# A transformer block on one core: the last batch's attention in two passes over the queries, and a new set of planning constants

## The chip, the cores and the metric

The kernel runs on one core of a Trainium2 chip. The metric is the device time of one execution, in microseconds (us); less is better. TensorE is called PE, VectorE DVE, ScalarE ACT, GpSimd POOL and SyncE SP, as in the profile. All DMAs but the indirect ones are issued from SP's queue; the indirect gathers and scatters are issued from POOL's.

## The reference, cut to what matters

Input x is 8 batches of 1024 tokens with 256 features. Per batch: layer norm, causal attention with 16 heads of 16 features, in which every value row is scaled by a gate computed from its token (a small network), output projection and residual; then layer norm and a mixture of experts (8 experts of 128 hidden units, 2 of them chosen per token by a grouped gate, and a shared expert of 256 hidden units) with its residual.

```python
Q = (x @ Wq + bq); K = (x @ Wk + bk); V = (x @ Wv + bv)        # 16 heads of 16
logits = einsum('bqhd,bkhd->bhqk', Q, K) * scale               # causal
attn = softmax(logits); gated = attn * gate[:, None, None, :]
x = x + einsum('bhqk,bkhd->bqhd', gated, V) @ Wo + bo
...
h = silu(x @ w1[e]) * (x @ w3[e]);  y = sum_e ew[t, e] * h @ w2[e]
shared = silu(x @ sg) * (x @ su) @ sd;  out = x + y + shared
```

## The kernel before

**A list scheduler writes the order.** `plan_work` adds items: each has an engine, an estimated duration, a due time, the items it needs, PSUM banks and, on PE, a tiling (`FULL`, `ROWS`, `COLS`). `Plan.run` simulates the engines greedily: of the items of an engine that can start now it takes the one with the least due time, with `SAME_TILING` added to the due time of an item that would change PE's tiling, and it never leaves an engine idle for an item that comes later. The result is a fixed order of instructions for each engine. Items of one kind (the two letters of their name) keep the order in which they were added. `LATER` shifts the due times of whole kinds; `SWITCH` and `EXPOSED` are charged to PE items. These numbers never reach the chip: only the order does.

**Attention.** The 16 heads go in 4 groups of 4, the queries in 2 chunks of 512 (c = 0 and 1). For a group and chunk: `LD` loads stacked queries and keys from DRAM (`load_stacks`, L965); `M` computes scores on PE (L1908) only to find each row's maximum with `MR` on DVE (L1549); `MT`, `MN` and `SM` turn, negate and move the maxima into the query stack (L1928, L1340, L972); `QK` computes transposed scores (L1941), `EX` exponentials on ACT (L1358), `MK` clears the causal corner on POOL (L1175), `PV` multiplies with the values on PE (L1961), `OE` and `SO` copy and store the sums (L1369, L978). Chunk 0 sees keys 0 to 511 and needs 5 scores items of the 18 of a group, all of them on the diagonal; chunk 1 sees all keys and needs 13. Every batch runs group by group, chunk 0 then chunk 1. There are 4 query halves (`Q_HALVES`) and 5 key halves (`K_HALVES`) in SBUF; chunk 1 uses the key half that chunk 0 loaded together with its own. The load of a group's chunk waits for the scores of the same chunk two groups before.

**Feed-forward.** The attention output of a batch is taken in quarters of 256 tokens. Once all four groups have stored a chunk, `CL`, `CR` and `CV` invert the softmax sums (L986, L1561, L990); then for each quarter `CO` loads (L1004 to L1007), `CP` scales on POOL (L1184, L1185), `CW` projects (L1970), a layer norm follows, `CT` transposes (L1978) and `CG` computes the gate (L1993). A unit of the feed-forward is `EU` (12 or 6 matmuls, L2071), `HT` (2 transposes, L2081) and `ED` (6 matmuls, L2102), with ACT and DVE work between them. In batches 0 to 6 a quarter runs 2 units (the shared expert), and the chosen experts run as units over tokens gathered by expert (`pair`: `XL` L1023, `XT` L2034, `YC` L1448, `YS` L1033), and `mix` brings them back: `RL` L1042, the two gathers `GY` on POOL (L1219), `CM` on ACT (L1294), `CB` and `CC` on POOL (L1227, L1232), `SY` L1046. The last batch has nothing behind it to hide this in, so its quarters run all 10 units densely: 40 units in all. `quarter_due`, `pairs_due` and `mix` give the due times; `LOOKS` sorts quarters and pairs into the one order in which their units run.

Around the end, then, the order is: the last batch's group 3, chunk 0, then chunk 1; its quarters 0 and 1 (tokens of chunk 0) and 2 and 3 (chunk 1); in between, the pairs of batch 6 and the mixing of batches 4 to 6.

Of the kernel before, what the change touches and what calls it, by code (L numbers as in the profile page):

```python
# [13 lines left out]
P = 128  # L14
B, S, E = 8, 1024, 256
H, DH = 16, 16
KE = E // P
# [49 lines left out]
LAST_MAX = [max(u for u in range(NMAX) if MAXU[u][0] == c) for c in range(CHUNKS)]  # L67
FFN_CHUNKS = 6
# [30 lines left out]
Q_HALVES, K_HALVES = 4, 5  # L99
ROWS_OF_HEAD = 64  # L100
# [9 lines left out]
SWITCH, EXPOSED = 100, 90  # L110
PERIOD, KEEPS = 3413, 0.58
SAME_TILING = 12000
# [9 lines left out]
FIRST = 50_000  # L122
SHARE_FROM, SHARE_TO, PAIRS_FROM, MIX_LONG = 0.12, 0.5, 0.72, 0.15
# [6 lines left out]

def quarter_due(n, q):
    return at(n + 1) + T * (SHARE_FROM + (SHARE_TO - SHARE_FROM) * q / QS)
# [45 lines left out]
def max_parts(u):  # L178
# [3 lines left out]
    for qt in qts:  # L182
# [7 lines left out]
LATER = {"AC": 8000, "AQ": -1000, "AX": 7000, "CB": 6000, "CC": -41000, "CG": 3000, "CJ": 2000, "CL": -8000,  # L190
# [33 lines left out]
class Plan:  # L224
# [16 lines left out]
    def run(self):  # L241
# [10 lines left out]
        while left:  # L252
# [76 lines left out]
def plan_work():  # L329
# [8 lines left out]
    def step_due(n, g, s):  # L338
        return at(n, g) + GROUP_T * step_at[s] // step_at[NSTEP]
# [66 lines left out]
    def values(n, g):  # L406
        add("POOL", ("VA", n, g), 1437, at(n, g) - 4000, [("PK", K_HALVES), ("GL", n), ("PV", n - 1, g, NSTEP - 1)])

    def maxima(n, g):
        gi = n * GROUPS + g  # L410
        older = divmod(gi - 2, GROUPS)
        begin = at(n, g) - GROUP_T * 0.98
        for c in range(CHUNKS):
            m = g // (GROUPS // KE)
            add("SP", ("LD", n, g, c), 4 * ISSUE, begin - GROUP_T * (1.0 - 0.3 * c),
# [13 lines left out]
            if c:  # L429
                add("DVE", ("MJ", n, g), 95, due, last)  # L430
                last = [("MJ", n, g)]
# [1713 lines left out]
```

## Time and profile before

| | |
|---|---|
| median of 3 runs | 1799.14 us (1796.13 to 1805.52) |
| the profiled execution | 1808.59 us, its span 1806.6 us |
| PE busy | 1653.0 us (91%) |
| DVE busy | 1292.4 us (72%) |
| ACT busy | 1081.9 us (60%) |
| POOL busy | 811.8 us (45%) |
| mean granted TensorE clock | 0.962 of full speed |

Busy time is the union of an engine's instructions. The chain of waits is followed back from the last instruction; windows are stretches of the span, counted from its start.

### The profile page before, as it was taken

To read this page: it belongs to the slowest core of one execution; us is meant where nothing else is said; L and a number is where in the kernel's file an instruction comes from. 1 tells how busy PE (TensorE), PEld (TensorE's weight loads), DVE (VectorE), ACT (ScalarE), POOL (GpSimd) and SP (SyncE) were. 2 spreads that over 40 slices of the span, in tenths; PEclk is the share of its full clock that TensorE was granted. 3 is DMA by queue.
4 is the path that set the end of the run, shared out by engine and by line. 5 is a ranking of instruction groups with operands and counts; after the bars stand their busy time and mean duration, and the time that the engine had idled before them with its cause. 6 is when DMAs were issued, how large, how long until landed. Compare 5 with 4: busy or idle time off the path is not lost.

```text
span 1806.6 us, 34673 instructions
## 1 busy us (share of the span) xinstructions
PE 1653.0 (91%) x12785; PEld 982.5 (54%) x12785; DVE 1292.4 (72%) x2528; ACT 1081.9 (60%) x1808; POOL 811.8 (45%) x1390
## 2 busy tenths in 40 slices
PE   7798989989988999899998989999999889999888
PEld 3344446435544566455654555555564557666677
DVE  5776767967795777777785757877688666963655
ACT  3466756665655655675656755586556765568432
POOL 5234533463345221632237863363207773157760
PEclk9699999999998999999998999999999999999999
DMA  5556655554445532644545665453535675336440
GB/s 151 158 156 194 176 169 152 182 153 124 125 127 147 158 104 87 174 113 120 159 118 151 185 194 152 127 162 108 147 93 172 198 197 159 97 129 199 135 122 13
DMA packets 192708, 261.25 MB, mean 145 GB/s; under 512 B 19616, under 2 KB 127264, under 8 KB 192544
## 3 DMA queue, kind: packets, MB, share of 16 engines
q1 hardware_dynamic: 181792, 229.67, 44.0%
q0 software_dynamic: 10752, 29.37, 5.6%
q8 instruction: 105, 1.72, 0.4%
q14 instruction: 59, 0.48, 0.1%
HBM read 130.98 MB, written 127.40 MB: 143 GB/s over the span
## 4 chain that ended last, share of the span: by engine, by line
PE 54%; DVE 14%; DMA 8%; ACT 8%; POOL 8%; issue 5%; SPq 3%; another core or an unknown queue 0%; POOLq 0%; ACTq 0%; DVEq 0%
PE ps_all L1961 10%; PE ps_all L2071 10%; DVE mx L1549 7%; PE ps_all L1941 6%; PE ps_all L1908 6%; PE ps_all L2102 5%; PE ps_all L1892 4%; ACT probs L1358 4%; PE ps_all L1878 3%; PE ps_all L1970 3%; POOL xs_s L1207 2%; PE ps_all L2081 2%; PE ps_all L2034 1%; DMA rr<-r_s 1%; DMA out<-rr 1%
## 5 line engine op out<-in xcount | busy, mean ns | idle before, releaser
L1549 DVE TENSOR_REDUCE mx<-ps_all 128x2 f32<-128x1024 f32 (+2 forms) x640 | 619.0, 1006 | 132.5 <-PE ps_all L1908 74.4
L1358 ACT ACTIVATE probs<-ps_all 128x1024 f32<-128x1024 f32 x576 | 571.8, 1028 | 218.0 <-PE ps_all L1941 209.9
L1175 POOL TENSOR_SCALAR_AFFINE_SELECT probs<-probs 128x256 f32<-128x256 f32 (+1 forms) x448 | 190.9, 443 | 495.5 <-ACT probs L1358 491.3
L1961 PE MATMUL ps_all<-probs,vaug 128*32 128x512 f32 (+3 forms) x3072 | 319.4, 516 | 21.9 <-POOL probs L1175 15.3
L1908 PE MATMUL ps_all<-k_st,q_st 63*128 63x512 f32 (+3 forms) x1536 | 269.3, 401 | 48.0 <-ACT probs L1358 16.3
L1941 PE MATMUL ps_all<-q_st,k_st 64*128 64x512 f32 (+3 forms) x1536 | 265.6, 401 | 29.3 <-ACT probs L1358 9.9
L1908 PEld LDWEIGHTS ps_all<-k_st,q_st 63*128 63x128 f32 x1536 | 135.1, 193 | 163.7 <-issue 52.2
L1941 PEld LDWEIGHTS ps_all<-q_st,k_st 64*128 64x128 f32 x1536 | 130.9, 191 | 158.9 <-issue 67.2
L2071 PE MATMUL ps_all<-w_hi,x2h 128*128 128x512 f32 (+1 forms) x480 | 168.2, 350 | 4.3 <-DVE x2l L1598 2.5
L1804 DVE SCALAR_TENSOR_TENSOR act_t<-act_t,ps_all 128x256 f32<-128x256 f32 x168 | 70.4, 419 | 123.4 <-ACT act_t L1421 110.9
L2071 PE MATMUL ps_all<-w_lo,x2h 128*128 128x512 f32 (+1 forms) x480 | 157.0, 327 | 0.0
L2071 PE MATMUL ps_all<-w_hi,x2l 128*128 128x512 f32 (+1 forms) x480 | 157.0, 327 | 0.0
L1421 ACT ACTIVATE act_t<-ps_all 128x256 f32<-128x256 f32 x168 | 64.6, 385 | 151.3 <-PE ps_all L2071 122.2
L1961 PEld LDWEIGHTS ps_all<-probs,vaug 128*32 128x32 f32 x3072 | 73.2, 110 | 131.6 <-issue 89.4
L1207 POOL DMA_INDIRECT xs_s<-xnb,slot_u x112 | 111.6, 996 | 42.9 <-issue 39.8
L1219 POOL DMA_INDIRECT yab<-ys_s,slot_u x112 | 108.3, 967 | 33.0 <-issue 20.2
L2102 PE MATMUL ps_all<-w_hi,h_hi 128*128 128x256 f32 (+1 forms) x336 | 109.5, 326 | 7.7 <-DVE h_lo L1831 6.9
L2071 PEld LDWEIGHTS ps_all<-w_hi,x2h 128*128 128x128 f32 x480 | 90.8, 189 | 27.6 <-issue 19.7
L1878 PE MATMUL ps_all<-wvd,xt 128*128 128x384 f32 x256 | 96.9, 506 | 1.8 <-issue 0.9
L2071 PEld LDWEIGHTS ps_all<-w_hi,x2l 128*128 128x128 f32 x480 | 90.9, 189 | 8.4
L1831 DVE TENSOR_TENSOR h_lo<-ps_all,h_hi 128x256 fp32r<-128x256 f32 x168 | 70.0, 419 | 35.1 <-ACT h_hi L1436 32.7
L2102 PE MATMUL ps_all<-w_lo,h_hi 128*128 128x256 f32 (+1 forms) x336 | 94.3, 281 | 0.0
(195 smaller groups left out, 2849.8 us busy)
## 6 DMA issues: line engine op xcount, KB each, us to landing
qk_s<-qh SPq DMA_DIRECT2D x116, 256.0 KB
q_st<-qk_s SPq DMA_DIRECT2D x128, 192.0 KB
k_st<-qk_s SPq DMA_DIRECT2D x128, 192.0 KB
xs<-xs_s SPq DMA_DIRECT2D x72, 256.0 KB
ys_s<-ysb SPq DMA_DIRECT2D x72, 256.0 KB
o_s<-o_sb SPq DMA_DIRECT2D x64, 256.0 KB
qk_s<-ql SPq DMA_DIRECT2D x57, 256.0 KB
xs_s<-ysb SPq DMA_DIRECT2D x20, 512.0 KB, 6.0
```

What stands on the lines that cost most here:

```text
L1175: last = nc.gpsimd.affine_select(out=block, in_=block, compare_op=ALU.is_ge, fill=0.0, base=0, pattern=[[0, heads], [1, P]], channel_multi ...
L1207: nc.gpsimd.indirect_dma_start(xs_s[i % 2], bass.IndirectOffsetOnAxis(ap=slot_u[:, n % 4, a, t:t + 1], axis=0), xnb[:, t, :], None).then_i ...
L1219: nc.gpsimd.indirect_dma_start(yab[:, t % 2, a, :], None, ys_s[SET_OF[n] % 2], bass.IndirectOffsetOnAxis(ap=slot_u[:, n % 4, a, t:t + 1], ...
L1358: nc.scalar.activation(to, of, ACT.Exp, scale=DH ** -0.5).then_inc(freed[release[item][0]], 1)
L1549: last = nc.vector.tensor_reduce(to[:, :, p, qt % QPC], both[:, :, at:at + keys], X_AXIS, ALU.max)
L1878: last = mm(bank(item)[:, 0:E + DP], xt[:, k, tt * P:(tt + 1) * P], wvd[:, k, :], start=(k == 0), stop=(k == KE - 1))
L1892: last = mm(bank(item), w[:, k, m * P:(m + 1) * P], xt[:, k, :], start=(k == 0), stop=(k == KE - 1))
L1908: last = mm(bank(item, j)[:, to:to + keys], q_st[r, q_half(n, g, c), p, qt % QPC * P:(qt % QPC + 1) * P], k_st[r, k_half(n, g, kc), p, 0:k ...
L1941: last = mm(bank(item, j)[:, to:to + cols], k_st[r, k_half(n, g, kt // QPC), a, kt % QPC * P:(kt % QPC + 1) * P], q_st[r, q_half(n, g, c), ...
L1961: last = mm(bank(first)[32 * h:32 * h + 32, q0 - c * CHUNK:], vaug[:, kt, g, h * VW:h * VW + 32], probs[:, s % 2, h, at:at + cols], start= ...
L2071: last = mm(bank(item)[:, to], x[:, buf, k, t * P:(t + 1) * P], w[:, k, cs], start=(k == 0 and j == 0), stop=(k == KE - 1 and j == 2))
L2102: last = mm(bank(first)[:, t * E:(t + 1) * E], h[:, z % 2, i * P:(i + 1) * P], w[:, cs], start=(item == first and i == 0 and j == 0), stop ...
```

## The change

1. The last batch's attention goes over chunk 0 of all four groups first, then over chunk 1 of all four. The list of (batch, group, chunk) in the new order is `VISITS`; all counters that semaphores are compared with are taken from positions in it.
2. In the last batch chunk 1 can no longer use the keys of chunk 0 where they were, so its load fetches both halves: 6 DMAs in place of 4 for each of 4 visits. `FREED_BY` names the visit whose scores must be done before a load may overwrite its buffers.
3. Quarters 0 and 1 of the last batch get earlier due times (`EARLY_FROM`, `EARLY_STEP`), and so does the inversion of their softmax sums.
4. The planner's costs change (`SWITCH`, `EXPOSED` and where they are charged, `SAME_TILING`), and `LATER` is replaced by a table with 91 kinds in place of 42.

```diff
+VISITS = ([(n, g, c) for n in range(B - 1) for g in range(GROUPS) for c in range(CHUNKS)]
+          + [(B - 1, g, c) for c in range(CHUNKS) for g in range(GROUPS)])
+VISIT_NO = {visit: v for v, visit in enumerate(VISITS)}
+STEP_NO, SCORE_NO, MASK_NO, MAX_NO = {}, {}, {}, {}
+for n, g, c in VISITS:
+    for s in range(FIRST_STEP[c], LAST_STEP[c] + 1):
+        STEP_NO[n, g, s] = len(STEP_NO)
+        for p in range(SCORES[s]):
+            SCORE_NO[n, g, s, p] = len(SCORE_NO)
+            if DIAGONAL[s]:
+                MASK_NO[n, g, s, p] = len(MASK_NO)
+    for u in range(NMAX):
+        if MAXU[u][0] == c:
+            MAX_NO[n, g, u] = len(MAX_NO)
+STEP_AT = list(STEP_NO)
...
+KEYS = [(v, kc) for v, (n, g, c) in enumerate(VISITS) for kc in range(c if n < B - 1 else 0, c + 1)]
+KEY_NO = {}
+for v, (n, g, c) in enumerate(VISITS):
+    for kc in range(c + 1):
+        KEY_NO[v, kc] = KEYS.index((v, kc) if (v, kc) in KEYS else (VISIT_NO[n, g, kc], kc))
+
+
+def freed_by(v):
+    last = {}
+    for (w, _), k in KEY_NO.items():
+        if w < v:
+            last[k % K_HALVES] = max(last.get(k % K_HALVES, 0), w)
+    own = [k % K_HALVES for k, (w, _) in enumerate(KEYS) if w == v]
+    return max([v - Q_HALVES] + [last.get(k, -1) for k in own])
+
+
+FREED_BY = [freed_by(v) for v in range(len(VISITS))]
...
-SWITCH, EXPOSED = 100, 90
+SWITCH, EXPOSED = 130, 60
 PERIOD, KEEPS = 3413, 0.58
-SAME_TILING = 12000
+SAME_TILING = 7000
...
+EARLY_FROM, EARLY_STEP = 0.95, 0.1
...
+def visit_at(n, g, c):
+
+    first = sum(SCORES[:FIRST_STEP[1]])
+    if n < B - 1:
+        return at(n, g) + c * GROUP_T * first // NSCORE
+    return at(n) + (c * T * first + g * GROUP_T * (NSCORE - first if c else first)) // NSCORE
+
+
 def quarter_due(n, q):
+    if n == B - 1 and q < QS // CHUNKS:
+        return at(n) + T * (EARLY_FROM + EARLY_STEP * q)
...
-LATER = {"AC": 8000, "AQ": -1000, "AX": 7000, "CB": 6000, "CC": -41000, "CG": 3000, "CJ": 2000, "CL": -8000,
...
+LATER = {"AB": 8000, "AC": 29000, "AE": 15000, "AG": -53000, "AN": 7000, "AQ": -1000, "AR": 26000, "AS": 46000,
...
                 if tile != tiling:
-                    ns += SWITCH + EXPOSED * (tile != COLS)
-                    tiling = tile
-                elif idle and tile != COLS:
-                    ns += min(EXPOSED, idle)
+                    ns, tiling = ns + SWITCH, tile
+                elif item[0] not in ("PV", "ED"):
...
+        load = begin - GROUP_T * (1.0 - 0.3 * c)
+        if n == B - 1:
+            begin = visit_at(n, g, c) - GROUP_T * (0.75 if c else 0.6)
+            load = begin - GROUP_T * 0.4
+        m = g // (GROUPS // KE)
+        user = FREED_BY[v]
+        free = [("QK",) + VISITS[user][:2] + (LAST_STEP[VISITS[user][2]], SCORES[LAST_STEP[VISITS[user][2]]] - 1)] if user >= 0 else []
+        add("SP", ("LD", n, g, c), (4 + 2 * (n == B - 1 and c)) * ISSUE, load,
+            [("PK", min(v + 1, K_HALVES - 1)), ("SQ", n, c, 2 * m), ("SQ", n, c, 2 * m + 1)] + free,
+            lands=9000 if n else 5000)
+        units = [u for u in range(NMAX) if MAXU[u][0] == c]
...
             early = at(n + 1) - (GROUP_T * 0.4 if c == 0 else 0)
+            if n == B - 1 and c == 0:
+                early = visit_at(n, 0, 1) + GROUP_T * 0.1
...
-        for g in range(GROUPS):
+        for g in range(GROUPS if n < B - 1 else 0):
             values(n, g)
-            maxima(n, g)
+            for c in range(CHUNKS):
+                maxima(n, g, c)
             if g + n * GROUPS:
                 pn, pg = divmod(n * GROUPS + g - 1, GROUPS)
                 for s in range(NSTEP):
                     attention(pn, pg, s)
-        if n:
+        if n and n < B - 1:
             rest(n - 1)
-    for s in range(NSTEP):
+    begun = VISIT_NO[B - 1, 0, 0]
+    for v in range(begun, len(VISITS)):
+        if v < begun + GROUPS:
+            values(*VISITS[v][:2])
+        maxima(*VISITS[v])
+        for n, g, c in VISITS[v - 2:v] if v == begun else VISITS[v - 1:v]:
+            for s in range(FIRST_STEP[c], LAST_STEP[c] + 1):
+                attention(n, g, s)
+    for s in range(FIRST_STEP[1], NSTEP):
         attention(B - 1, GROUPS - 1, s)
+    rest(B - 2)
     rest(B - 1)
...
-                if gi >= 2:
-                    sp.wait_ge(s_full, (gi - 2) * NSCORE + sum(SCORES[:LAST_STEP[c] + 1]))
-                cs = slice(c * CHUNK, (c + 1) * CHUNK)
-                for kind in range(2):
+                if FREED_BY[v] >= 0:
+                    on, og, oc_ = VISITS[FREED_BY[v]]
+                    sp.wait_ge(s_full, SCORE_NO[on, og, LAST_STEP[oc_], SCORES[LAST_STEP[oc_]] - 1] + 1)
+                for kind, part in [(0, c)] + [(1, kc) for w, kc in KEYS if w == v]:
+                    cs = slice(part * CHUNK, (part + 1) * CHUNK)
                     rows = qk_s[bass.ds(((n * 2 + kind) * H + g * GROUP) * TERMS, GROUP * TERMS), :]
                     rows = rows.rearrange("(p j r) s -> j r p s", j=2, r=TERMS)
                     for j in range(2):
                         r = slice(ROWS_OF_HEAD * j, ROWS_OF_HEAD * j + TERMS)
-                        to = q_st[r, q_half(n, g, c), :, :] if kind == 0 else k_st[r, k_half(n, g, c), :, :]
+                        to = q_st[r, q_half(n, g, c), :, :] if kind == 0 else k_st[r, k_half(n, g, c, part), :, :]
                         sp.dma_start(to.bitcast(F32), rows[j][:, :, cs]).then_inc(st_in[gi % 2][c], 16)
```

## Rows read from the trace of the kernel before

**Rows 1.** The page: busy time of each engine, share and instructions.
```profile
PE 1653.0 (91%) x12785; PEld 982.5 (54%) x12785; DVE 1292.4 (72%) x2528; ACT 1081.9 (60%) x1808; POOL 811.8 (45%) x1390
```
**Rows 2.** Windows: stretch, its length, busy of each engine (instructions), clock, DMA.
```profile
100.00:1455.00 1355.00, 1259.02 (x10011) 711.73 (x10009) 1002.49 (x1867) 846.72 (x1347) 593.68 (x1014) 0.97 0.52 148
1455.00:1660.00 205.00, 193.04 (x1635) 131.82 (x1635) 141.70 (x269) 136.68 (x247) 105.24 (x155) 0.99 0.53 155
```
**Rows 3.** Windows, the same columns, ten us each around the two gaps.
```profile
1660.00:1670.00 10.00, 7.28 (x55) 4.65 (x55) 2.35 (x6) 5.43 (x11) 6.73 (x9) 0.90 0.59 173
1670.00:1680.00 10.00, 5.14 (x27) 3.37 (x26) 2.02 (x7) 3.98 (x8) 7.04 (x11) 0.84 0.60 159
1680.00:1690.00 10.00, 9.08 (x39) 6.59 (x39) 6.17 (x19) 3.29 (x10) 6.21 (x7) 0.75 0.56 179
1690.00:1700.00 10.00, 8.53 (x46) 6.72 (x45) 7.84 (x31) 5.36 (x15) 8.18 (x12) 1.00 0.31 95
...
1740.00:1750.00 10.00, 6.52 (x21) 4.21 (x22) 2.24 (x7) 3.50 (x9) 6.55 (x10) 0.66 0.58 172
1750.00:1760.00 10.00, 8.09 (x43) 6.50 (x42) 8.54 (x28) 2.48 (x7) 4.17 (x4) 1.00 0.15 51
1760.00:1770.00 10.00, 10.00 (x55) 8.74 (x54) 6.13 (x21) 3.81 (x11) 1.07 (x3) 0.83 0.01 2
```
**Rows 4.** Timeline of PE at the first gap: start, length, instructions, idle before.
```profile
1672.40 0.64 PE L1961 MATMUL ps_all<-probs,vaug 128*32 128x256 f32 x8
1672.97 1.13 PE L1970 MATMUL ps_all<-wo,oc 128*128 128x256 f32 x4
1678.96 1.18 PE L1978 MATMUL ps_all<-ident,xnb 128*128 128x128 f32 x4 [4.86 <-ACT xnb L1315]
...
1682.31 0.63 PE L2071 MATMUL ps_all<-w_hi,x2h 128*128 128x512 f32 x1
```
**Rows 5.** Chain of waits near the end: start, length, what.
```profile
1790.60 1.37 PE ps_all L2071 x6
1791.97 0.22 PE ps_all L2081 x2
1792.19 0.71 PE ps_all L2102 x6
1792.90 1.38 PE ps_all L2071 x6
```
**Rows 6.** Timeline of SP: stores of the last batch's sums, and the loads after them.
```profile
1457.55 0.47 SPq L978 DMA_DIRECT2D o_s<-o_sb  x1
1475.16 0.58 SPq L978 DMA_DIRECT2D o_s<-o_sb  x1
1522.80 0.43 SPq L978 DMA_DIRECT2D o_s<-o_sb  x1
...
1625.49 0.33 SPq L978 DMA_DIRECT2D o_s<-o_sb  x1
1638.80 0.33 SPq L978 DMA_DIRECT2D o_s<-o_sb  x1
...
1673.72 0.32 SPq L978 DMA_DIRECT2D o_s<-o_sb  x1
1686.97 0.61 SPq L990 DMA_DIRECT2D li_s<-rows_of  x1
```
**Rows 7.** Timeline of SP: from quarter 0's sums to its loads.
```profile
1652.07 0.60 SPq L990 DMA_DIRECT2D li_s<-rows_of  x1
1655.86 0.64 SPq L1004 DMA_DIRECT2D oc<-o_s  x1
```
**Rows 8.** Timeline of POOL: quarter 0's and quarter 3's scaling.
```profile
1666.87 1.27 POOL L1184 TENSOR_TENSOR oc<-oc,lb 128x512 f32<-128x512 f32 x1
...
1754.22 1.34 POOL L1184 TENSOR_TENSOR oc<-oc,lb 128x512 f32<-128x512 f32 x1
```
**Rows 9.** Timeline of SP: group 3's stacks loaded, its last maxima moved.
```profile
1573.63 0.80 SPq L965 DMA_DIRECT2D q_st<-qk_s  x2
1574.48 0.90 SPq L965 DMA_DIRECT2D k_st<-qk_s  x2
...
1617.48 1.32 SPq L972 DMA_DIRECT2D q_st<-rows_of  x2
```
**Rows 10.** The page, costliest groups: maxima on DVE.
```profile
L1549 DVE TENSOR_REDUCE mx<-ps_all 128x2 f32<-128x1024 f32 (+2 forms) x640 | 619.0, 1006 | 132.5 <-PE ps_all L1908 74.4
```
**Rows 11.** Timeline of PE: a feed-forward unit cut by attention scores.
```profile
1659.65 0.28 PE L2071 MATMUL ps_all<-w_hi,x2l 128*128 x1
1659.86 0.50 PE L1941 MATMUL ps_all<-q_st,k_st 64*128 64x384 f32 x4
1660.29 0.39 PE L2102 MATMUL ps_all<-w_hi,h_hi 128*128 x1
```

More of the change, by code:

```diff
@@ L406, in values, with maxima @@
     def values(n, g):
-        add("POOL", ("VA", n, g), 1437, at(n, g) - 4000, [("PK", K_HALVES), ("GL", n), ("PV", n - 1, g, NSTEP - 1)])
-    def maxima(n, g):
+        add("POOL", ("VA", n, g), 1437, visit_at(n, g, 0) - 4000, [("PK", K_HALVES), ("GL", n), ("PV", n - 1, g, NSTEP - 1)])
+    def maxima(n, g, c):
         gi = n * GROUPS + g
         older = divmod(gi - 2, GROUPS)
+        v = VISIT_NO[n, g, c]
         begin = at(n, g) - GROUP_T * 0.98
-        for c in range(CHUNKS):
-            m = g // (GROUPS // KE)
-            add("SP", ("LD", n, g, c), 4 * ISSUE, begin - GROUP_T * (1.0 - 0.3 * c),
-                [("PK", min(gi * CHUNKS + c + 1, K_HALVES - 1)), ("SQ", n, c, 2 * m), ("SQ", n, c, 2 * m + 1), ("QK",) + older + (LAST_STEP[c], SCORES[LAST_STEP[c]] - 1)],
-                lands=9000 if n else 5000)
-            units = [u for u in range(NMAX) if MAXU[u][0] == c]
-            for u in units:
-                _, p, kc, qts = MAXU[u]
-                blocks = len(qts) * (1 if p is not None else PAIRS)
-                due = begin + GROUP_T * 0.9 * u / NMAX
-                add("PE", ("M", n, g, u), 240 if kc < c else 310 if blocks == 1 else 445, due,
-                    [("BT",), ("LD", n, g, c), ("MT",) + older + (c,)], 2, ROWS)
-                add("DVE", ("MR", n, g, u), sums(2 * sum(part[1] for part in max_parts(u)) * blocks // len(qts)) + 65 * len(qts), due + 1000, [("M", n, g, u)],
-                    frees=(("M", n, g, u), None))
-            due += 1500
-            last = [("MR", n, g, units[-1])]
-            if c:
-                add("DVE", ("MJ", n, g), 95, due, last)
-                last = [("MJ", n, g)]
-            add("PE", ("MT", n, g, c), 60, due, last, 1, FULL)
-            add("ACT", ("MN", n, g, c), 160, due, [("MT", n, g, c)] + ([("SM",) + divmod(gi - 1, GROUPS) + (c,)] if gi else []),
-                frees=(("MT", n, g, c), None))
-            add("SP", ("SM", n, g, c), 2 * ISSUE, due, [("MN", n, g, c)], lands=2600)
@@ new lines, in maxima @@
+        units = [u for u in range(NMAX) if MAXU[u][0] == c]
+        for u in units:
+            _, p, kc, qts = MAXU[u]
+            blocks = len(qts) * (1 if p is not None else PAIRS)
+            due = begin + GROUP_T * 0.9 * (u - units[0] * (n == B - 1)) / NMAX
+            add("PE", ("M", n, g, u), 240 if kc < c else 310 if blocks == 1 else 445, due,
+                [("BT",), ("LD", n, g, c), ("MT",) + older + (c,)], 2, ROWS)
+            add("DVE", ("MR", n, g, u), sums(2 * sum(part[1] for part in max_parts(u)) * blocks // len(qts)) + 65 * len(qts), due + 1000, [("M", n, g, u)],
+                frees=(("M", n, g, u), None))
@@ L437, in attention @@
+        due += 1500
+        last = [("MR", n, g, units[-1])]
+        if c:
+            add("DVE", ("MJ", n, g), 95, due, last)
+            last = [("MJ", n, g)]
+        add("PE", ("MT", n, g, c), 60, due, last, 1, FULL)
+        add("ACT", ("MN", n, g, c), 160, due, [("MT", n, g, c)] + ([("SM",) + divmod(gi - 1, GROUPS) + (c,)] if gi else []),
+            frees=(("MT", n, g, c), None))
+        add("SP", ("SM", n, g, c), 2 * ISSUE, due, [("MN", n, g, c)], lands=2600)
     def attention(n, g, s):
@@ L1954, in sums @@
                 if DIAGONAL[s]:
-                    pe.wait_ge(p_masked, gi * MASKS + sum(SCORES[i] for i in range(s + 1) if DIAGONAL[i]))
+                    pe.wait_ge(p_masked, MASK_NO[n, g, s, SCORES[s] - 1] + 1)
                 else:
```

69 lines of the change are left out of this document (34 added, 35 removed), and 16 rows, old and new, of the table LATER.

## The prediction

> **What bounds the kernel now.** The page's list of busy times comes first: PE is busy 91% of the span, the next engine, DVE, 72% [rows 1]. So PE's work is the bound as long as something is ready for it, and time is lost only where PE waits or runs at its low clock. Windows over long stretches say where: from 100 to 1455 us PE is idle for 1355 - 1259 = 96 us, from 1455 to 1660 us (nearly all of the last batch's attention) for 12 us only, at a granted clock of 0.99 [rows 2]. Windows of ten us behind that show two gaps. From 1660 to 1700 us PE is idle for 2.7 + 4.9 + 0.9 + 1.5 = 10.0 us, and the granted clock falls to 0.75 of full, so a part of it at 1.2 instead of 2.4 GHz; from 1740 to 1770 us it is idle for 3.5 + 1.9 = 5.4 us with the clock down to 0.66 [rows 3]. The clock's share is roughly (1 - clock) times the busy time of each row: 0.7 + 0.8 + 2.3 = 3.8 us in the first, 2.2 + 1.7 = 3.9 us in the second. Together the two gaps cost 10.0 + 5.4 + 3.8 + 3.9 = 23.1 us.
>
> The timeline shows what the first one is. The last PV of the attention and the projection of quarter 0 end at about 1674 us; then PE has nothing for 4.86 us, until ACT's normalised rows of quarter 0 arrive, and quarter 0's first dense unit begins at 1682.3 us [rows 4]. All 40 dense units of the last batch lie behind the attention. Once they flow they repeat every 2.31 us (1790.60 to 1792.90) with PE full: 1.37 us of EU, 0.22 of HT, 0.71 of ED [rows 5]. Nothing in the units themselves can be shortened by an order; only the gaps can.
>
> Quarters 0 and 1 need only chunk 0 of the four groups. Its last store is issued at 1638.8 us, because group 3's chunk 0 comes so late [rows 6].
>
> **The change, part by part.**
>
> *The order of the last batch.* The stores of sums, taken in turn (chunk 1 of batch 6, then chunks 0 and 1 of batch 7's groups), give the length of a visit: 17.6 us for group 0's chunk 0 and 47.6 for its chunk 1, 34.9 for group 3's chunk 1; over the whole, 1673.7 - 1457.6 = 216 us, or 54 a group, of which 5/18 = 15 is chunk 0 and 13/18 = 39 chunk 1 [rows 6]. With all chunks 0 first, they are done at 1457.6 + 4 x 15 = about 1518 us, 120 us before the present 1638.8. Quarters 0 and 1 can then run anywhere from about 1550 us on: 20 units, 46 us of PE work, that need not wait for the end. PE's amount of work does not shrink by this. What it can give back is the gaps: both lie where the chain of a quarter (load, scaling, projection, norm, gate) ran with no unit ready, and now 20 units can stand there. I take all of the 23.1 us as removed, and count what is late next as a term of its own.
>
> *Idle time within the attention.* 12 us of it are left [rows 2], and a unit that is ready can fill such holes: 5 units at most. Bounds 0 and -12; the holes are short and spread, nearest to half: -6.
>
> *What is late next: quarters 2 and 3.* They still need the very last chunk. From the last PV (1673.0) to the inverted sums' store (1687.0 + 0.6) are 14.6 us [rows 4, 6]; from quarter 0's such store to its first load 3.8 us [rows 7]; from there to its scaling on POOL 11.0 us [rows 7, 8], some of which is POOL busy with the mixing (lower bound 7); from the scaling to the first unit 1682.3 - 1666.9 = 15.4 us [rows 4, 8]. The chain is 41 to 45 us. It must be covered by units of quarters 0 and 1 that are still unspent. Their due times (0.95 and 1.05 of the batch's length) stand just before and just behind the attention's last steps, so the planner gives attention the first place and spends units early only where PE would idle, about 5. 15 x 2.31 = 35 us of cover remain, and the last pairs of batch 6 add a little. Uncovered: 41 to 45 minus 35, 6 to 10 us; with the clock's fall behind such a gap (nearly 4 us of 14 in the first one) and a few us covered by pairs, I take +9. If no unit were left it would be over 40; this is the first rival below.
>
> *Keys loaded twice, and their buffers.* 4 visits issue 6 loads in place of 4; two take 0.90 us of SP's queue [rows 9], so 3.6 us of issue in all, spread over 150 us in which SP has long pauses: nothing, and if that cover were gone, under 1 us a visit. Behind these two on SP stand the moves of maxima and the stores of sums, which would be late by the same 0.9 us. The wait matters more. Two key halves a visit in a ring of 5 means that a visit's load waits for the scores of the visit two before. Up to now a chunk 1 load could be issued 54 + 15 = 69 us before its scores were due; now, 39 us (34.9 for the last ones). Group 3's load and the last move of its maxima stand 1617.5 - 1573.6 = 44 us apart, unhurried [rows 9]; the least is 13 maxima of 1.006 us on DVE [rows 10] plus about 10 us for load, turn and move, 25 us in all (this 10 is an estimate from the pieces of the chain above: each pass through DRAM took 4 to 8 us). So the chain fits if DVE gives it priority, and is late by up to 10 us a visit if it does not. While it is late PE still has units. Bounds 0 and +15; I take +3, nearest to the row of 25 us needed against 35 given.
>
> *Switches of tiling.* Dense units ran unbroken behind the attention; among scores and values PE changes its tiling around each piece. In the row where a unit's last matmul (pace 0.12 us) is followed by scores, about 0.1 us goes at each of the two changes [rows 11]. A unit has 3 pieces, so at most 6 changes, 0.6 us. For 5 to 8 units +3 to +5; for all 20, +12; I take +4, since the due times leave most units behind the attention.
>
> The Trainium skill bears on this place. TensorEngine Tiling (Array Packing), Key Properties, says that a change of tiling mode drains TensorE, and names no price. The row above shows such a boundary at about 0.1 us; by the row the sum is the one below; by a drain that every piece pays in full it would be that of the rival on switches.
>
> *Costs and due times of the whole plan.* The first seven batches are reordered as well, with no change of work. Here the trace shows only the pool: 96 us of idle PE between 100 and 1455 us [rows 2]. One thing can be tested: the old charges add to 1370 + 140 + 692 = 2202 ns for a unit without idle time, the new ones to 2322, and the trace has 2.31 us [rows 5]. The new charges describe a full PE better, so an order made by them has a fair chance to be better on the chip; but a table of shifts up to 87 us is fitted to the planner, not to the chip. Bounds -20 (a fifth of the idle time) and +20; I take -5, near to nothing.
>
> **The sum.** -23.1 - 6 + 9 + 3 + 4 - 5 = -18 us. Against the profiled execution, 1808.6 us, that is 1790.6, or -1.0%. That execution lies 9.5 us above the median of the runs shown, 1799.1, so the same share gives a median of 1781 us.
>
> **The rivals.**
>
> *The cover is spent too early* (the slower side). Batch 7 has no projections of a next batch to fill PE with, and the planner is greedy: each stall in the chunk 1 visits takes a unit. With k units left at the last PV, 45 - 2.31 k us are exposed, and the sum is -23 - 12 + 45 + 2 (clock) + 3 + 12 (switches of 20 units) - 5 (retuning) - 2.31 k = 22 - 2.31 k. It decides from k = 9.5: fewer left is slower than before. With 4 left, +13: 1812. For it: the units are ready at 1550 us, 120 us early. Against it: only 12 us of idle time are there to take them [rows 2], and their due times. Chance 0.13.
>
> *The key ring stalls each chunk 1 visit.* Three visits late by 5 us that units do not fill: +15 in place of +3: -6, so 1793. For it, 44 us unhurried against 35; against it, DVE's 72%. Chance 0.14.
>
> *Every unit pays dear switches.* All 20 units spread over the attention, each of 6 changes at twice the row's 0.1 us: +24 in place of +4, with the idle time filled whole, -12 in place of -6. The sum is -4, 1795. For it, that the row shows a boundary only where the next weights were at hand; against it, that attention and pairs mix in this way already at 94% busy [rows 2]. Chance 0.10.
>
> *The retuning is worth more than the order.* -20 in place of -5: -33, 1766. For it, 96 us of idle PE that an order could use. Chance 0.15.
>
> *The change does not do what it says*: quarters 0 and 1 are due but held by POOL, whose gathers and additions for the mixing stand before the scaling (it ran at 1666.9 though its loads were issued at 1655.9 [rows 7, 8]). Then the tail stays as it was and only the retuning is left, around 1799 and on either side of it. Chance 0.08.
>
> **How the numbers follow.** The forecast, 1781, has a chance of 0.40 with a range of its own from 1770 to 1792. Faster and slower by 0.5% (9 us, about what a measurement here tells from no change) are below 1790 and above 1808. Faster: most of the forecast's 0.40 (0.36), the retuning 0.15, half of the ring's and the switches' together 0.12, a little of the others 0.04: 0.67. Slower: the spent cover 0.10, the last rival and the bad side of the retuning 0.05: 0.15. The rest, 0.18, is no change. The range for 8 in 10 goes from 1757, the retuning rival and its own spread, to 1806, where the ring, the switches and the unchanged tail lie within it and most of the spent cover does not.
>
> **What would show it.** In the trace after: the last store of chunk 0 near 1520 us in place of 1638.8; dense units (L2071 in its form with 6 matmuls) before the last PV; PE's idle time between the last PV and the end under 12 us; a single gap, if any, in front of quarter 2's first unit; the load of a chunk 1 visit issued right after the scores of the visit two before, and PE at 0.94 or more busy there. A gap of over 20 us behind the last PV would show the first rival; PE or ACT waiting for the move of the maxima the second; PE busy time up by 10 us with no new idle time the third; the same gaps with the end earlier, the fourth.

## The result: slower by 1.5%, and the profile after

The changed kernel takes 1827.57 us in the median of 4 runs (1820.24 to 1834.68); the kernel before, run beside it, 1800.97 us. The ratio is 1.0146 [1.0112, 1.0181]. The forecast was 1781, the range ended at 1806, and the chance given to slower was 0.15. The profiled executions lie closer together than the medians: 1820.2 us after and 1808.6 before, so the two traces hold only 12 of the 27 us by which the medians differ.

The page of the changed kernel, busy times, answers to [rows 1]:

```profile
PE 1650.7 (91%) x12726; PEld 980.8 (54%) x12726; DVE 1284.9 (71%) x2528; ACT 1085.6 (60%) x1808; POOL 813.1 (45%) x1390
```

PE does the same work in both kernels; what was added is idle time: 14 us, while its busy time fell by 2. Windows of the changed kernel (stretch, length, busy time of PE, PEld, DVE, ACT and POOL with instructions, granted clock, DMA share, GB/s): up to the last batch's first sums, from there to its last PV, and the tail.

```profile
0.00:1462.00 1462.00, 1331.15 (x10344) 747.91 (x10344) 1048.27 (x1971) 890.13 (x1408) 636.23 (x1146) 0.96 0.51 147
1462.00:1702.00 240.00, 215.15 (x1758) 144.71 (x1757) 162.19 (x329) 151.49 (x279) 133.39 (x192) 0.99 0.52 156
1702.00:1819.00 117.00, 104.40 (x634) 88.21 (x632) 74.41 (x229) 44.01 (x123) 43.44 (x54) 0.97 0.28 87
```

The same three stretches of the kernel before:

```profile
0.00:1457.00 1457.00, 1336.03 (x10455) 750.20 (x10455) 1067.97 (x1986) 892.93 (x1420) 640.04 (x1153) 0.96 0.52 148
1457.00:1673.00 216.00, 202.38 (x1695) 138.04 (x1695) 143.23 (x275) 140.70 (x255) 112.52 (x164) 0.98 0.53 155
1673.00:1807.00 134.00, 114.62 (x640) 94.26 (x636) 81.25 (x268) 48.23 (x135) 59.29 (x75) 0.93 0.29 88
```

Length minus PE's busy time is its idle time. The tail lost 17 us of length and 6.8 of idle time (19.4 to 12.6), as a change of that kind should do. The attention before it grew by 24 us, of which 11.2 is idle time (13.6 to 24.9) and the rest units that moved into it. So the last batch takes 7 us more as a whole, and the first seven batches 5. Those 5 say too little: fewer matmuls lie in that stretch (10344 records against 10455), and PE's idle time in it grew by 10 us, from 121.0 to 130.9. So the seven batches whose attention order nobody meant to change hold a large part of the new idle time. This pair of traces cannot say where the other 15 us of the medians are; runs side by side on one chip could.

SP's timeline of the changed kernel (start, length, queue, line, transfer, count) answers to [rows 6, 7]; "..." marks rows left out:

```profile
1534.44 0.34 SPq L1046 DMA_DIRECT2D o_s<-o_sb  x1
...
1702.33 0.32 SPq L1046 DMA_DIRECT2D o_s<-o_sb  x1
...
1715.90 0.60 SPq L1058 DMA_DIRECT2D li_s<-rows_of  x1
...
1723.98 0.39 SPq L1082 DMA_DIRECT2D out<-x  x1
...
1726.24 0.62 SPq L1072 DMA_DIRECT2D oc<-o_s  x1
```

The first row is the last store of a chunk 0, at 1534 us in place of 1639; the second the last store of a chunk 1. The last three are the store of chunk 1's inverted sums, which quarters 2 and 3 need, the store of quarter 0's result, and quarter 2's first load; they come back below.

### The profile page after: what moved, and what is told of

The parts are those of the page before. It is cut to its first block, busy times and chain, and to the rows that moved or that the text cites. A ratio compares the mean times of both kernels' runs of the same rounds, so it can differ in the third digit from the quotient of the medians.

```text
span 1818.4 us, 34577 instructions
## 1 busy us (share of the span) xinstructions
PE 1650.7 (91%) x12726; PEld 980.8 (54%) x12726; DVE 1284.9 (71%) x2528; ACT 1085.6 (60%) x1808; POOL 813.1 (45%) x1390
## 4 chain that ended last, share of the span: by engine, by line
PE 46%; DMA 13%; DVE 12%; ACT 9%; POOL 7%; SPq 6%; issue 5%; another core or an unknown queue 1%; POOLq 0%; DVEq 0%; ACTq 0%
PE ps_all L2136 9%; PE ps_all L2026 8%; PE ps_all L2167 5%; DVE mx L1614 5%; PE ps_all L2006 5%; PE ps_all L1973 5%; ACT probs L1425 4%; PE ps_all L1957 4%; DMA qk_s<-ql 3%; POOL xs_s L1275 2%; PE ps_all L1943 2%; PE ps_all L2035 2%; PE ps_all L2146 2%; SPq L1004 1%
## 5 line engine op out<-in xcount | busy, mean ns | idle before, releaser
L2026 PE MATMUL ps_all<-probs,vaug 128*32 128x512 f32 (+3 forms) x3072 | 319.0, 510 | 16.3 <-POOL probs L1243 12.7
L2026 PEld LDWEIGHTS ps_all<-probs,vaug 128*32 128x32 f32 x3072 | 70.6, 110 | 118.0 <-issue 80.5
L1501 ACT CAST h_hi<-ps_all 128x256 fp32r<-128x256 f32 x168 | 62.1, 372 | 80.6 <-PE ps_all L2146 74.9
```

What stands on the lines that cost most here:

```text
L2026: last = mm(bank(first)[32 * h:32 * h + 32, q0 - c * CHUNK:], vaug[:, kt, g, h * VW:h * VW + 32], probs[:, STEP_NO[n, g, s] % 2, h, at:at ...
```

## Experiments

Two theories stood at the start. **A**: the new constants made a worse order of the first seven batches. **B**: the loss is in the last batch, from its order or its key ring. Neither had it alone, and **C** came after the first four runs: a detail of the new due times that seemed to change nothing. **D** and **E** are about one wait of the tail, and come last. Each kernel ran 4 to 10 times. Ratios are to the kernel before on the same chip, with a 95% interval; they are estimated from the runs and are not the quotients of the two medians. The kernels of one heading shared a chip. Code cuts leave lines out where "..." stands.

### First chip (the kernel before: 1791.66 us)

`e1` is the new order with the old charges and shifts.

```diff
-SWITCH, EXPOSED = 130, 60
+SWITCH, EXPOSED = 100, 90
...
-SAME_TILING = 7000
+SAME_TILING = 12000
...
-                elif item[0] not in ("PV", "ED"):
...
+                elif idle and tile != COLS:
...
```

The table `LATER` is the old one of 42 kinds again.

> The new order of the last batch with the old planning constants: SWITCH, EXPOSED and SAME_TILING and the table LATER are those of the kernel before. Theory A (the loss lies in the new constants, which reorder all eight batches; the order of the last batch is a gain): 1780 to 1795 us against 1801, last store of attention sums before 1685 us. Theory B (the order of the last batch itself loses, through the ring of five key halves: PE runs dry in front of the last chunk 1 visit): 1810 to 1830, the last store near 1700.

Measured: 1804.18 us, 1.0063 [1.0032, 1.0094]. Slower, but by less than half of the loss, and in the range of neither theory.

`e2` is the opposite: the kernel before, only with the new charges, `SAME_TILING` and table.

> The old order of the last batch with the new charges and the new table LATER. Theory A: slower than before, 1810 to 1825. Theory B: within 0.5% of before or faster, 1785 to 1808. The end of batch 6's attention (store of its last sums), 1457.6 us before and 1462.4 after the change, lies near 1462 in both.

Measured: 1767.76 us, 0.9882 [0.9841, 0.9922]. The constants alone were faster here, so A fell; that they were faster by this much neither theory had said. (The size did not come back on two other chips, e9 and e15 below.)

`e3` is the changed kernel with the old table `LATER` and the new charges.

> The changed kernel with the old table LATER, but the new charges (SWITCH, EXPOSED, SAME_TILING). Theory A: if the table is what loses, near e1_reorder_only; if the charges are, near the changed kernel, 1820 to 1830. Theory B: near the changed kernel, and again a wait of PE for the maxima of a chunk 1 visit.

Measured: 1806.32 us, 1.0088 [1.0061, 1.0115]. Not to be told apart from e1: without the new table the loss is as small as without all new constants, although e2 shows no loss from the table by itself.

`e4` is e1 without the double load: in the last batch chunk 1 loads one key half and uses it for both, so its scores come from keys partly not the right ones, with the same instructions on PE. The lines that follow from this one (which half is read, what is waited for, the planned length of the load) change with it.

```diff
-KEYS = [(v, kc) for v, (n, g, c) in enumerate(VISITS) for kc in range(c if n < B - 1 else 0, c + 1)]
+KEYS = [(v, c) for v, (n, g, c) in enumerate(VISITS)]
...
```

> As e1_reorder_only, but in the last batch chunk 1 loads one key half and uses it in place of both (wrong keys, same matmuls, 4 DMAs a visit in place of 6), so that the ring of five is no limit: the load may be issued as soon as the queries' buffer is free. Theory A: within 4 us of e1. Theory B: 8 to 15 us faster than e1, with the last chunk 1 visits 35 to 39 us long and no wait of PE for a maximum.

Measured: 1797.29 us, 1.0025 [1.0003, 1.0047]; against e1 0.4% or 7 us less, the intervals just overlapping. In the profiles the stretch of attention shrinks from 245 to 236 us and the tail is 108 us in both. So the key ring probably costs something, between the +3 of the forecast and the +15 of the second rival, though not clear of noise; the planned order of the last batch differs between e1 and e4 too. Both theories' ranges (within 4 us, 8 to 15 us) were missed.

### Second chip (1800.24 us): the rounding

That A and B were each too small left what e1, e3, e4 and the changed kernel share and e2 has not. The new function of due times adds up two integer divisions where one stood:

```diff
-        return at(n, g) + GROUP_T * step_at[s] // step_at[NSTEP]
+        c = STEPS[s][0]
+        return visit_at(n, g, c) + GROUP_T * (step_at[s] - step_at[FIRST_STEP[c]]) // step_at[NSTEP]
```

For batches 0 to 6 the two mean the same time, but two divisions round down twice: for `QK` of batch 0, step 4, it gives 73332 ns where it was 73333. So 768 of the attention's 1792 score, exponential, mask and PV items, all in chunk 1's steps, become due 1 ns earlier. What follows was worked out from the plans of e2 and e6, which have the new constants and differ in nothing else. The first order that differs is a tie in batch 0: score item (0, 0, 8, 1) is taken on PE ahead of the maxima item (0, 1, 13), not behind it. From there the greedy planner goes another way through all batches: 1592 of PE's 2503 items stand in another place (by 4.3 places in their mean, 72 at most), 1313 of DVE's 2136. Making all `M` items due 1 ns later has exactly the same effect.

The planner's own simulation shows the loss as well: its last item starts at 1645.0 us in e2's plan and at 1661.6 in e6's, at 1649.4 with exact due times (e7) and 1668.5 in the changed kernel. And it shows that this is no even draw. Moving the due time of one kind at a time by 1000 ns either way lengthens e2's plan in 41 of the 44 cases that change its length, by 8.9 us in the median, and shortens the changed kernel's in 36 of 44. So the new constants look fitted to the exact due times, and the rounding takes the plan off that fit. These are plans and were not run. With the old constants the rounding lengthens the plan less, from 1671.0 to 1675.4 us.

`e5` puts that rounding, and nothing else, into the kernel before; `e6` puts it into e2.

```diff
-        return at(n, g) + GROUP_T * step_at[s] // step_at[NSTEP]
+        first = step_at[FIRST_STEP[STEPS[s][0]]]
+        return at(n, g) + GROUP_T * first // NSCORE + GROUP_T * (step_at[s] - first) // NSCORE
```

> The kernel before with one thing of the change: the due times of the attention steps are computed with the new formula's two whole-number divisions in place of one, which makes those of a third of the attention items 1 ns smaller. Ties in the list scheduler then fall otherwise, and from 74 us of the plan on the order of all batches is another one. Theory C (much of the loss is this reshuffle, which nobody chose): 8 us or more away from before, near e1_reorder_only (0.6% slower). Theory B (the last batch's order is the loss): within 0.3% of before.

Measured: 1810.47 us, 1.0060 [1.0040, 1.0080]. With the old constants the rounding alone costs 0.6%, all that e1 lost.

> As e2_retune_only (new charges and table, old order of the last batch), with the new formula's rounding, 1 ns in a third of the due times. Theory C: well above e2's ratio of 0.988, 1.000 or more, so that only the rest to 1.0146 is the last batch's order. Theory B: 0.988 within 0.3%.

Measured: 1819.61 us, 1.0117 [1.0057, 1.0177]. With the new constants it comes to most of the whole loss (e2, its partner, ran on another chip; the pair on one chip is e9 and e11).

`e7` takes it out of the changed kernel by the edit below; `e8` also gives quarters 0 and 1 and their inversion the old due times.

```diff
     def step_due(n, g, s):
         c = STEPS[s][0]
+        if n < B - 1:
+            return at(n, g) + GROUP_T * step_at[s] // step_at[NSTEP]
         return visit_at(n, g, c) + ...
```

> The changed kernel with the old formula for the due times of batches 0 to 6, so that its order is the one of e2_retune_only until near the end of batch 6, and differs only by the new order of the last batch. Theory C: a large part of the way from 1.0146 back to e2's 0.988, 0.995 or less. Theory B: 1.010 or more, with the same waits in the last batch as after the change.

Measured: 1792.78 us, 0.9966 [0.9940, 0.9991].

> As e7_after_exact, but quarters 0 and 1 of the last batch have their old due times, behind the attention. If interleaving quarter 0 with the attention costs (it delays the last chunk 1 visits), 3 to 8 us faster than e7; if it fills holes as forecast, slower by as much. The order of visits is the same in both.

Measured: 1790.15 us, 0.9945 [0.9923, 0.9966]. One added `if` in the planner (e7), without any arithmetic on the chip changed, turns 1.5% slower into a little faster. No effect of the early due times is seen: the intervals of e7 and e8 overlap, though by the plans 6 units of quarter 0 begin ahead of the last PV in e7 and none in e8.

### Third chip (1803.61 us): two by two

All four have the new constants; old or new formula for batches 0 to 6, old or new order of the last batch. e9 is e2 again, e10 is e7, e11 is e6, e12 the changed kernel.

> The kernel of e2 once more, so that the four corners (formula old or new, order of the last batch old or new, all with the new constants) stand on one chip with the same runs of before. Theory C (the reshuffle is the loss): 0.988 of before again. If e2 owed its time to its chip: 0.993 or more.

> The kernel of e7 once more: old formula, new order of the last batch. Theory C: 0.997 of before; its distance to e9, some 0.8%, is then the price of the new order of the last batch. If that price came from the chips, under 0.4% from e9.

> The kernel of e6 once more: new formula, old order of the last batch. In the plan one tie is broken otherwise, at 80.2 us of PE's order, between the last maxima of group 1 and a score of group 0 in batch 0; everything that differs follows from it. Theory C: 1.010 to 1.015 of before.

> The changed kernel itself beside the other three: 1.010 to 1.018 of before. If the two parts add up, its distance to e11 is that of e10 to e9.

| measured | old order of the last batch | new order |
|---|---|---|
| exact due times | e9: 1800.96, 0.9990 [0.9966, 1.0015] | e10: 1800.2, 0.9976 [0.9946, 1.0007] |
| rounded twice | e11: 1827.05, 1.0131 [1.0083, 1.0178] | e12: 1824.15, 1.0111 [1.0055, 1.0167] |

Down a column it is 1.4% (1.0131 / 0.9990, 1.0111 / 0.9976), 24 to 26 us; along a row 0.1 to 0.2%, not to be told from nothing. C held, and the whole loss is in the reshuffled order. Two of the numbers named with it did not: 0.988 for e9, as on the chip of e2, and a price of 0.8% for the new order (e10 against e9).

Where it goes is read from e9 and e11, which differ in nothing but the order. Windows of e9: to the end of batch 4, batches 5 and 6, the last batch's attention, the tail.

```profile
0.00:1021.00 1021.00, 929.97 (x7231) 509.06 (x7231) 753.50 (x1398) 626.30 (x972) 433.69 (x823) 0.96 0.52 149
1021.00:1445.00 424.00, 392.19 (x3111) 234.78 (x3113) 309.79 (x583) 265.33 (x441) 204.21 (x328) 0.97 0.52 150
1445.00:1674.00 229.00, 209.87 (x1742) 143.83 (x1738) 145.29 (x283) 146.02 (x262) 116.69 (x171) 0.97 0.50 146
1674.00:1800.00 126.00, 111.50 (x640) 91.23 (x640) 80.99 (x265) 49.38 (x137) 57.26 (x71) 0.97 0.31 95
```

The same of e11:

```profile
0.00:1027.00 1027.00, 931.71 (x7197) 510.42 (x7198) 745.62 (x1396) 624.02 (x967) 434.31 (x820) 0.96 0.51 148
1027.00:1476.00 449.00, 410.04 (x3181) 245.31 (x3181) 311.88 (x586) 271.14 (x450) 204.18 (x332) 0.94 0.49 142
1476.00:1706.00 230.00, 203.87 (x1715) 138.67 (x1713) 145.13 (x283) 143.00 (x258) 118.47 (x172) 0.96 0.49 146
1706.00:1827.00 121.00, 109.21 (x640) 89.85 (x638) 82.17 (x263) 49.13 (x136) 56.52 (x69) 0.99 0.32 97
```

6 us are lost by the end of batch 4 and 25 in batches 5 and 6; behind them 4 come back. The lengths alone mislead a little, since some work moved into batches 5 and 6 from both sides (3181 records of PE against 3111). Over the whole, PE's idle time grows by 15.7 us: 4.3 by the end of batch 4, 7.1 in batches 5 and 6, 7.0 in the last batch's attention, and 2.7 less in the tail. Its busy time grows by 11.3 us, with a granted clock of 0.94 in place of 0.97 in batches 5 and 6, which is a longer time for the same kinds of work. No single wait carries the loss of batches 5 and 6: PE's waits there are 4.9 us at most, and 4.8 in e9. What in the order costs stays open.

The tie itself, at 88.5 us, in PE's timeline of e9, where the maxima (L1913, L1921) go first, and of e11, where the scores (L1947) do:

```profile
88.46 0.51 PE L1913 MATMUL ps_all<-k_st,q_st 63*128 63x512 f32 x2
88.80 0.24 PE L1921 MATMUL ps_all<-bars 64*128 64x64 bf16 x4
88.87 0.48 PE L1946 MATMUL ps_all<-q_st,k_st 64*128 64x384 f32 x4
```

```profile
89.27 0.50 PE L1947 MATMUL ps_all<-q_st,k_st 64*128 64x384 f32 x4
89.61 0.45 PE L1914 MATMUL ps_all<-k_st,q_st 63*128 63x512 f32 x2
89.90 0.23 PE L1922 MATMUL ps_all<-bars 64*128 64x64 bf16 x4
```

Each is about 1 us of work either way. The exchange itself costs nothing; what the planner makes of it does.

Why the new order gained nothing is read from e9 and e10. Windows of e10, the last three stretches:

```profile
1028.00:1445.00 417.00, 387.24 (x3121) 234.14 (x3119) 303.27 (x579) 266.08 (x444) 204.17 (x329) 0.99 0.53 153
1445.00:1685.00 240.00, 216.86 (x1725) 145.43 (x1726) 162.14 (x325) 147.25 (x270) 128.54 (x185) 0.95 0.52 153
1685.00:1802.00 117.00, 105.75 (x634) 88.69 (x633) 76.81 (x229) 45.99 (x125) 45.24 (x56) 0.97 0.29 88
```

PE's idle time from 1445 us on is 19.1 + 14.5 = 33.6 us in e9 and 23.1 + 11.3 = 34.4 in e10, and the two stretches take 355 and 357 us. The idle time has moved from the tail into the attention.

### Fourth chip (1797.40 us): a wait of the tail

The trace of the changed kernel has quarter 2's sums stored at 1715.90 us but its load issued only at 1726.24, behind the store of quarter 0's result at 1723.98. The residual rows have two buffers, so a quarter waits for the store of the quarter two before. **D** says that this is on the path; **E** that it is not. `e13` is e8 again; `e14` is e13 with the residual rows of quarters 2 and 3 in a projection buffer that is idle by then; `e15` is e2 again and `e16` is e15 with that same buffer. By the plans the order of PE in each pair is the same up to the last units of quarter 0, so e14 and e16 change the tail alone. The cut shows two of the places; the scaling, the norm and the store take the same buffer.

```diff
+        def x1_of(n, q):
+            return xa[:, q % 2, :, :] if n == B - 1 and q > 1 else x1[:, q % 2, :, :]
...
-                if k >= 2:
+                if n == B - 1 and q > 1:
+                    sp.wait_ge(a_xn, B * TILES)
+                elif k >= 2:
                     sp.wait_ge(r_st[buf], k // 2 * 16)
```

> The kernel of e8 again (new constants, old formula, new order of visits, quarters 0 and 1 due behind the attention), as the base of e14 on the same chip: 0.995 of before.

> As e13, but quarters 2 and 3 of the last batch keep their residual rows in the projection's idle input buffer, so that quarter 2's load need not wait until quarter 0 is stored. Theory D (the expected gain was given back there: the load of quarter 2 waited 29 us on quarter 0's store in e8, behind its inverted sums): 5 to 10 us less than e13, PE idle time behind the last PV under 8 us. Theory E (it went to the longer chunk 1 visits): within 3 us of e13.

> The kernel of e9 again, as the base of e16 on the same chip: 0.99 to 1.00 of before, and within 0.5% of e13.

> As e15 (old order of the last batch), with the spare residual buffers of e14. Theory D: here the same wait stood behind quarter 0 too (its sums were ready 27 us before its load), so 4 to 8 us less than e15 and a version that beats both kernels: 0.985 to 0.993 of before. Theory E: within 3 us of e15.

| | without | with the buffer |
|---|---|---|
| new order | e13: 1796.82, 0.9982 [0.9955, 1.0009] | e14: 1787.99, 0.9957 [0.9935, 0.9979] |
| old order | e15: 1793.71, 0.9983 [0.9961, 1.0005] | e16: 1789.89, 0.9957 [0.9923, 0.9991] |

SP's timelines, of e13 and then of e14: the sums' store, the result's store in e13, and quarter 2's load.

```profile
1683.21 0.60 SPq L1056 DMA_DIRECT2D li_s<-rows_of  x1
...
1709.78 0.39 SPq L1080 DMA_DIRECT2D out<-x  x1
...
1712.25 0.63 SPq L1070 DMA_DIRECT2D oc<-o_s  x1
```

```profile
1680.93 0.60 SPq L1059 DMA_DIRECT2D li_s<-rows_of  x1
...
1684.01 0.63 SPq L1075 DMA_DIRECT2D oc<-o_s  x1
```

The load came 29 us behind the sums, and now 3. The tails of e13 and of e14:

```profile
1670.00:1793.00 123.00, 111.82 (x647) 92.72 (x646) 83.16 (x266) 48.07 (x136) 52.09 (x65) 0.97 0.28 87
```

```profile
1667.00:1783.00 116.00, 108.86 (x654) 91.85 (x652) 83.08 (x266) 48.54 (x137) 52.27 (x65) 1.00 0.30 92
```

7 us shorter, 4.0 of them idle time, the rest the clock that no longer falls. The medians agree in direction in both pairs (8.8 and 3.8 us), and the ratios fall by 0.25% or 4.5 us in each; the intervals overlap, so D is supported by the trace and by two like differences, not proven to size. e16's 0.9957 misses what D had forecast for it (0.985 to 0.993). It also shows that the wait is no price of the new order: the old one gains as much without it. e14 and e16 are the only versions of this chip whose interval excludes 1. e8's 0.9945 did not come back in e13, the same kernel, nor e2's 0.9882; what is left against the kernel before is 0.3 to 0.6%.

## Why the prediction was wrong

**The term that failed is the last one, costs and due times of the whole plan.** It was taken as -5 with bounds of 20 either way. Measured: the constants -0.1 and -0.2% (e9, e15; -1.2% on the chip of e2, not repeated), near to nothing as taken; but the new formula of due times +26 us (e11 against e9), which makes the part as a whole +23 us (e11 against the kernel before) and +19 on the second chip (e6), close to the upper bound and beyond it. The prediction said that the first seven batches are reordered "with no change of work" and asked what new constants would do. It did not compare `step_due` with its predecessor for unchanged batches, and the upper bound had nothing behind it but symmetry. The row that it quoted could have warned it: 96 us of idle PE [rows 2] is what one greedy order left, and another may leave more. The planner itself gave a hint: by its simulation the changed kernel ends only 2 us before the kernel before (1668.5 against 1671.0), where e2's plan ends 26 us before it (1645.0). Those 26 us came on the chip of e2 (24) and not on the other two (3 and 4). So the simulation put the plans with the new constants in about the measured order (e2, e7, e6 and the changed kernel), but not the changed kernel against the kernel before. "The retuning is worth more than the order" had 0.15; its bad side, which came true, was given a small part of 0.05.

**The two gaps, -23.1, and the idle time within the attention, -6.** Half right. The tail's idle time fell from 19.4 to 12.6 us and its clock rose from 0.93 to 0.97. But against -6 forecast for the attention there were +11.2 there, and with exact due times +4.0 (e10 against e9). PE was busy for 0.90 of that stretch, where the prediction had named 0.94. So the gains in the tail are real and are given back ahead of it.

**The order itself** came as told: the last chunk 0 is stored at 1534 us (forecast about 1520, before 1638.8). By the plan 6 units of the 20 begin ahead of the last PV, near the 5 forecast, and four units of batch 6's chosen experts went behind it. PE's timeline of the changed kernel at the last PV (L2026), with the pieces of dense units around it:

```profile
1700.70 0.38 PE L2146 MATMUL ps_all<-ident,act_t 128*128 128x128 f32 x2
1701.01 0.64 PE L2026 MATMUL ps_all<-probs,vaug 128*32 128x256 f32 x8
1701.58 0.50 PE L2136 MATMUL ps_all<-w_hi,x2h 128*128 128x512 f32 x1
```

PE does not stop there: the gap of 4.86 us in [rows 4] is gone. The first rival, the spent cover, was wrong; about 14 units stood behind the last PV, 32 us. Nor did the third, dear switches, happen: PE's busy time went from 1653.0 to 1650.7 us, not up by 10. The term of +4 is too small to be told apart in it.

**What is late next, +9.** One gap remains, in front of quarter 2's first unit, as forecast; a window of the changed kernel:

```profile
1740.00:1750.00 10.00, 10.00 (x69) 9.13 (x68) 5.79 (x17) 2.73 (x9) 0.00 (x0) 1.00 0.00 0
1750.00:1760.00 10.00, 6.43 (x28) 4.18 (x26) 3.04 (x10) 3.15 (x7) 3.55 (x6) 0.73 0.33 94
```

3.6 us of idle time and 0.27 x 6.43 = 1.7 us by the clock: 5.3, where +9 was taken. But the way there is another one. The chain from the last PV to quarter 2's first unit was put at 41 to 45 us, by the rows of quarter 0. Quarter 2 has one more thing to wait for, a semaphore that the prediction left out: its residual rows take the buffer of quarter 0, so its load waits until quarter 0 is stored. This was so in the kernel before, whose second gap lies behind it: the sums are stored at 1686.97 us [rows 6], and SP's timeline goes on with quarter 0's store and quarter 2's load, 34 us later:

```profile
1719.21 0.39 SPq L1014 DMA_DIRECT2D out<-x  x1
...
1721.43 0.61 SPq L1004 DMA_DIRECT2D oc<-o_s  x1
```

In the changed kernel the load comes 10.3 us behind the sums (1715.90 to 1726.24), in e13 29, and not 3.8 [rows 7]. In e13 PE takes the projection at 1724.17 us, as soon as the scaling is done (1722.82 and 1.30 us long), so a later load makes a later projection; e14 is the test of it. In the changed kernel the wait does not reach PE: POOL's scaling is early, and PE's fixed order has the projection 12 us later, behind units.

```profile
1733.31 1.29 POOL L1252 TENSOR_TENSOR oc<-oc,lb 128x512 f32<-128x512 f32 x1 [17.25 <-DMA x<-in_x]
```

```profile
1746.92 1.02 PE L2035 MATMUL ps_all<-wo,oc 128*128 128x256 f32 x4
```

The whole chain is 56 us long there (1701.6 to 1757.5), and units of quarters 0 and 1 and of batch 6 cover all but the gap.

**Keys loaded twice and their buffers, +3.** e4 puts it at 7 us, within the bounds. Group 3's load for chunk 1 is issued at 1610.92 us, right after PE's last scores of the visit two before (1610.88): the ring is the limit, as forecast. A late move of maxima, costed at under 1 us a visit, is seen in SP's timeline of the changed kernel. It is that of group 2:

```profile
1610.92 0.80 SPq L1033 DMA_DIRECT2D q_st<-qk_s  x2
1611.77 2.90 SPq L1033 DMA_DIRECT2D k_st<-qk_s  x4
...
1615.66 0.34 SPq L1046 DMA_DIRECT2D o_s<-o_sb  x1
...
1617.03 0.62 SPq L1072 DMA_DIRECT2D oc<-o_s  x1
...
1619.56 0.49 SPq L1075 DMA_DIRECT2D x<-in_x  x1
1620.10 1.35 SPq L1040 DMA_DIRECT2D q_st<-rows_of  x2
...
1663.69 1.31 SPq L1040 DMA_DIRECT2D q_st<-rows_of  x2
```

ACT had written the maxima by 1617.16 us (first fence below), but the move stands in the queue behind quarter 1's five loads and is issued at 1620.10. PE waits for it (second fence):

```profile
1616.89 0.27 ACT L1408 ACTIVATE rows_of<-ps_all 16x128 fp32r<-16x128 f32 x1 [0.39 <-PE ps_all L1993]
```

```profile
1624.99 2.08 PE L2006 MATMUL ps_all<-q_st,k_st 64*128 64x512 f32 x8 [8.13 <-DMA q_st<-rows_of]
```

8.13 us in one piece, of which 2.9 passed in the queue and 4.9 between the issue and PE's start. With it the clock falls, as the window shows:

```profile
1620.00:1630.00 10.00, 4.83 (x28) 2.79 (x32) 0.00 (x0) 5.26 (x8) 7.46 (x9) 0.66 0.66 200
```

It is 8.08 us in e12 too. But it is not the price of the double loads. e1 has the same doubled loads and early quarters, and what its scores waited for moves in the last batch's attention is 1.9 us in two waits (total, times, longest):

```profile
PE ps_all L2001 <- DMA q_st<-rows_of: 1.9, 2, 1.4
```

Nor do PE's longest waits there in e10 name a move. So this wait came with the changed kernel's planned order, that of the new constants and the rounding. Two things were left out of the prediction: the loads of the quarters, which the early order puts among the moves, and that the last visit's way from load to move would take 53 us (1610.92 to 1663.69) and not the 44 of [rows 9], let alone 25. The second rival, the key ring, was right in that the ring holds the loads back. Its price, 15 us in place of 3, was not reached by e4's 7, and it did not decide.

**The price of being right about the rest.** With exact due times the changed kernel is e7 and e10: 0.9966 [0.9940, 0.9991] and 0.9976 [0.9946, 1.0007]. Against the forecast of -1.0% a quarter to a third came. Of the rest, the ring may hold 7 us (by e4, with the old constants). Quarter 2's buffer, 4.5 to 9 us by e14 against e13, is not shown to hold any of it in e7 and e10: in e10's trace the load came only 7 us behind the sums, and PE took the projection 21 us after the scaling began. A kernel without both was not tried, so where the missing gain went stays open in part.

## What to carry to other kernels

In a kernel whose order comes from a greedy planner, an edit of a due time, even by 1 ns through a second rounding, can make another order of everything behind it: here it cost 1.4%, several times what the rest of the change was worth on the same chip. It is not a fair draw where the constants were fitted to the order that is lost: fit them to the formula they are used with. So compare the planned order of the stages that an edit should leave alone before pricing it, and hold them fixed when measuring; else the measurement is of the order. And when a stage is moved earlier, follow all the issues that it brings into a shared queue, and each buffer that one of its loads has to wait for.

## What was not expected of the hardware

The same kernel, old order with the new constants, stood at 0.9882 [0.9841, 0.9922], 0.9990 [0.9966, 1.0015] and 0.9983 [0.9961, 1.0005] of the kernel before on three chips. The first interval excludes the other two, so an interval of one chip does not cover what a change of order does on another. Whether the chip or the run did it was not told apart. The rounding went the same way on both chips where it was tried (e5 and e6, e11 and e12).

A wait of PE costs more than its length: in the window at 1620 us PE is idle for half of it and its granted clock is 0.66, so part of the work around it ran at 1.2 in place of 2.4 GHz. In e14's tail, with 7.1 us of idle time in place of 11.2, the clock stays at 1.00.
